# Head scores of a graph attention layer: four products into four banks instead of two pairs into two, with a new order of stages

## The reference

```python
x = _layernorm(x + L0(x, adj))   # one attention over the graph, softmax, elu
x = _layernorm(x + L1(x, adj))   # three times: attention, layer norm, feed-forward 256-1024-256 with gelu, layer norm
x = _layernorm(x + L2(x, adj))   # as L0, but only the 16 largest weights of each row are kept
x = _layernorm(x + L3(x, adj))   # eight heads of 32 features
```

```python
q, k, v = heads(x @ Wq), heads(x @ Wk), heads(x @ Wv)      # 8 heads, DK = 32
scores = einsum('bhnd,bhmd->bhnm', q, k) / sqrt(32)
scores = where(mask, scores, -inf)
out = einsum('bhnm,bhmd->bhnd', softmax(scores), v)
return relu(out) @ Wo
```

## Time and profile of the kernel before

| | |
|---|---|
| median of 3 timed runs | 4183.35 us (4180.52 to 4186.57) |
| profiled execution | 4172.75 us |
| its span, first to last instruction | 4171.1 us |
| mean granted TensorE clock | 0.927 |
| busy: TensorE, VectorE, ScalarE, GpSimd | 3650.7, 2396.8, 2176.5, 698.0 us |
| products of the heads' scores (L1183) | 1024 instructions, 315.6 us busy |
| transposes of the heads (L1195) | 2048 instructions, 360.8 us busy |

### The profile page before, as it was taken

One profiled execution on the slowest core, in us unless ns is written; L12 is line 12 of the kernel. 1 busy time (PEld: TensorE's weight loads), 2 busy tenths in 40 slices (PEclk: granted clock), 3 DMA queues, 4 the chain that ended last, 5 costly groups with the idle time before them and its releaser, 6 DMA issues.

```text
span 4171.1 us, 60266 instructions
## 1 busy us (share of the span) xinstructions
PE 3650.7 (88%) x18816; PEld 2758.4 (66%) x18816; DVE 2396.8 (57%) x6645; ACT 2176.5 (52%) x4321; POOL 698.0 (17%) x684
## 2 busy tenths in 40 slices
PE   6789898898988989899898998989898898998867
PEld 5676666766666676676766666666666766667653
DVE  3365564656656565565656656565565655646543
ACT  2255555455654555555554555555555554554623
POOL 1212121211111112121111212111121121212110
PEclk8799999998999999999999999989999998999987
DMA  4000000000000000000000000000000000000000
GB/s 120 1 6 6 6 11 7 11 1 6 11 7 11 6 2 10 7 11 6 6 6 7 11 6 11 4 4 11 6 11 7 6 6 6 11 6 1 1 5 6
DMA packets 42353, 39.73 MB, mean 10 GB/s; under 512 B 10016, under 2 KB 40992, under 8 KB 42016
## 3 DMA queue, kind: packets, MB, share of 16 engines
q1 hardware_dynamic: 33568, 27.17, 2.2%
q0 software_dynamic: 8448, 8.39, 1.4%
HBM read 35.55 MB, written 8.39 MB: 11 GB/s over the span
## 4 chain that ended last, share of the span: by engine, by line
PE 70%; issue 13%; DVE 8%; ACT 7%; POOL 2%; DVEq 0%; DMA 0%; ACTq 0%; POOLq 0%; SPq 0%
PE work L1133 16%; PE acc L1147 15%; PE acc L1111 11%; PE acc L1195 6%; PE work L1183 5%; PE work L1056 4%; PE work L1097 3%; PE acc L1213 2%; PE work L1162 2%; PE work L1026 2%; ACT PT L976 2%; PE work L1069 1%; DVE stats L692 1%; POOL rstd L477 1%; ACT T L907 1%
## 5 line engine op out<-in xcount | busy, mean ns | idle before, releaser
L1133 PE MATMUL work<-XT,w_sb 128*128 128x256 f32 x3072 | 759.2, 394 | 53.7 <-DVE XT L749 46.1
L477 POOL TENSOR_TENSOR rstd<-var_eps,minus_half 128x2 f32<-128x2 f32 x320 | 224.7, 702 | 3297.8 <-DVE var_eps L701 3297.8
L1147 PE MATMUL acc<-w_sb,gT 128*128 128x256 f32 x3072 | 716.6, 380 | 0.0
L1133 PEld LDWEIGHTS work<-XT,w_sb 128*128 128x128 f32 x3072 | 580.5, 196 | 182.9 <-DVE XT L749 44.4
L1147 PEld LDWEIGHTS acc<-w_sb,gT 128*128 128x128 f32 x3072 | 573.8, 190 | 85.1 <-issue 11.4
L947 ACT ACTIVATE gT<-work,b_sb 128x256 f32<-128x256 f32 x768 | 352.5, 473 | 365.9 <-PE work L1133 363.6
L1111 PE MATMUL acc<-X,PT 128*128 128x256 f32 x1536 | 392.6, 412 | 55.1 <-ACT PT L915 36.8
L1111 PEld LDWEIGHTS acc<-X,PT 128*128 128x128 f32 x1536 | 309.0, 207 | 128.1 <-issue 58.3
L810 DVE COPY PT<-acc 128x512 f32<-128x512 f32 x256 | 176.9, 691 | 292.3 <-PE acc L1195 288.1
L1183 PE MATMUL work<-X,R 32*128 32x512 f32 x1024 | 315.6, 663 | 19.3 <-DVE X L787 19.3
L976 ACT ACTIVATE PT<-acc 128x512 f32<-128x512 f32 x256 | 152.5, 596 | 297.2 <-PE acc L1195 295.2
(11 more groups left out here) (128 smaller groups left out, 5871.1 us busy)
## 6 DMA issues: line engine op xcount, KB each, us to landing
HX<-in_x SPq DMA_DIRECT2D x16, 512.0 KB, 3.9
pos<-in_adj POOLq DMA_DIRECT2D x16, 512.0 KB, 5.5
out<-X SPq DMA_DIRECT2D x32, 256.0 KB, 2.1
w_sb<-in_L_gnn_W SPq DMA_DIRECT2D x6, 1024.0 KB, 8.0
g_sb<-in_L_gnn_g SPq DMA_DIRECT2D x6, 128.0 KB, 5.1
c_sb<-in_L_gnn_beta SPq DMA_DIRECT2D x3, 128.0 KB, 4.1
PT<-in_L_gnn_b SPq DMA_DIRECT2D x3, 128.0 KB, 5.4
beta_sb<-in_L_gnn_beta SPq DMA_DIRECT2D x1, 384.0 KB, 7.8
```

The source lines that it names most:

```text
L477: pool.tensor_tensor(rstd[s][:, half_rows(half)], var_eps[s][:, half_rows(half)], minus_half[:], ALU.pow)\
L1133: last = pe.matmul(u.bank[:, 0:HN], w1_sb[:, l, c, f * P:(f + 1) * P], XT[s][:, c, half * HN:(half + 1) * HN], start=(c == 0), stop=(c == ...
L1147: last = pe.matmul(acc[s][half][:, i, :], gT[s][:, f, i * P:(i + 1) * P], w2_sb[:, l, f, :], start=(f == 0 and i == 0), stop=(f == FC - 1) ...
```

## The change

The 16 duos of a batch become 8 "quads" (`QUADS`, `NQ`): the four heads of a chunk for one tile of rows. Stage `sq{q}` multiplies all four into `acc[s][0]`, `acc[s][1]`, `work[s][0]`, `work[s][1]`; VectorE reads the first two banks in `sq{q}` and the other two in `sr{q}`. The four transposes of a quad go to the four banks as well, one each (`place_of` turns them by one where an output holds `acc[0]`). Each group of outputs has a bank use of its own, 256 columns: groups 0 to 2 in `acc[0]`, copied out by ScalarE with a Relu (`pc0` to `pc2`), group 3 in `acc[1]`. The spreading of the reciprocals comes at the end for both chunks (`rt0`, `rb0`, `rt1`, `rb1`); `rb0` is read by VectorE straight from its bank. A class `HeadUse` gives bank and semaphores for place 0 to 3.

```diff
-    DUOS = [(m, half, i, duo) for m in range(DC) for half in range(2) for i in range(HT) for duo in range(HPC // 2)]
+    QUADS = [(m, half, i) for m in range(DC) for half in range(2) for i in range(HT)]
...
+        for q in range(NQ):
+            uses += ([(f"scores {q + 1}", 2)] if q + 1 < NQ else []) + [(f"pT {q}", 2)]
+        uses += [("rden 1", 2)]
...
+        for q in range(NQ):
+            if q + 1 < NQ:
+                for h in range(2):
+                    acc_uses[h] += [(f"scores {q + 1}", 1)]
+            if q % 2 == 0 and q:
+                acc_uses[0] += [(f"outputs {q // 2 - 1}", 1)]
+            if q + 1 == NQ:
+                acc_uses[1] += [("rdenT 0", 1)]
+            for h in range(2):
+                acc_uses[h] += [(f"pT {q}", 1)]
+        acc_uses[0] += [("rden 0", 1), ("L3", 1)]
+        acc_uses[1] += [(f"outputs {GROUPS - 1}", 1), ("L3", 1)]
...
-        def bank_of(n):
-
-            return 1 if n < later else 0
+        def place_of(q, r):
+
+            return (r + 1) % HPC if q % 2 == 0 and q else r
...
+        class HeadUse:
+
+
+            def __init__(self, s, it, place, name):
+                if place < 2:
+                    self.bank = flat(acc[s][place])
+                    self.filled, self.filled_at = acc_filled[place].sems[s], acc_filled[place].value(it, name)
+                    self.evacuated, self.done = acc_evacuated[place].sems[s], acc_evacuated[place].value(it, name)
+                    self.free = acc_evacuated[place].value(it, name) - 1
+                else:
+                    u = Use(s, it, name, place - 2)
+                    self.bank, self.filled, self.filled_at = u.bank[:], u.filled, u.turn
+                    self.evacuated, self.free, self.done = u.evacuated, u.turn, u.turn + 1
...
+            def heads_normed(s, it, key):
+
+                last = Use(s, it, "rden 1", 1)
+                dve.wait_ge(last.evacuated, last.turn + 1)
+                outputs = HeadUse(s, it, 0, f"outputs {GROUPS - 2}")
+                dve.wait_ge(outputs.evacuated, outputs.done)
+                dve.tensor_tensor(XT[s][:, 1, 0:HN], XT[s][:, 1, 0:HN], chunks(R[s][:])[:, 1, 0:HN], ALU.mult)
+                use = HeadUse(s, it, 0, "rden 0")
+                dve.wait_ge(use.filled, use.filled_at)
+                dve.tensor_tensor(XT[s][:, 0, :], XT[s][:, 0, :], use.bank, ALU.mult).then_inc(use.evacuated, 1)
...
+            def group_outputs(g):
+                m, half = g // 2, g % 2
+
+                def stage(s, it, key):
+                    use = HeadUse(s, it, 0, f"outputs {g}")
+                    act.wait_ge(use.filled, use.filled_at)
+                    act.activation(XT[s][:, m, half * HN:(half + 1) * HN], use.bank[:, 0:HN], ACT.Relu).then_inc(use.evacuated, 1)
+                return stage
...
-                    for b in range(2):
-                        use = Use(s, it, f"scores d{d}", b)
-                        pe.wait_ge(use.evacuated, use.turn)
+                    places = [HeadUse(s, it, r, f"scores {q}") for r in range(HPC)]
+                    for use in places:
+                        pe.wait_ge(use.evacuated, use.free)
...
-                    for b in range(2):
-                        use = Use(s, it, f"scores d{d}", b)
-                        rows = slice((2 * duo + b) * DK, (2 * duo + b + 1) * DK)
-                        pe.matmul(use.bank[:], q_sb[s][rows, m, t * P:(t + 1) * P], k_sb[s][rows, m, :],
+                    for r, use in enumerate(places):
+                        rows = slice(r * DK, (r + 1) * DK)
+                        pe.matmul(use.bank, q_sb[s][rows, m, t * P:(t + 1) * P], k_sb[s][rows, m, :],
                                   start=True, stop=True).then_inc(use.filled, 1)
```

The list `HALF` is new as a whole. Its part with the heads, as it is now:

```diff
+        ("middle", "L1.0", "xsum1 xnorm1 xa1"), ("ending", "L3", "load qk0"), ("middle", "L1.1", "xT1"),
+        ("ending", "L3", "sq0"), ("middle", "L1.1", "s bc"), ("ending", "L3", "sr0"), ("middle", "L1.1", "zs0"),
+        ("ending", "L3", "v1"), ("middle", "L1.1", "mx0 zs1 exp0 mx1"), ("ending", "L3", "qk1"),
+        ("middle", "L1.1", "exp1 pT0"), ("ending", "L3", "ex0"), ("middle", "L1.1", "pT1"),
+        ("ending", "L3", "ex1 sq1 ex2 ex3"), ("middle", "L1.1", "agg0"),
+        ("ending", "L3", "sr1 uT0 ex4 uT1 ex5 uT2 ex6 uT3"), ("middle", "L1.1", "pT2 pT3"),
+        ("ending", "L3", "ex7 sq2 uT4"), ("middle", "L1.1", "sum0"), ("ending", "L3", "ex8 sr2"),
+        ("middle", "L1.1", "norm0"), ("ending", "L3", "uT5"), ("middle", "L1.1", "agg1"),
+        ("ending", "L3", "ex9 uT6"), ("middle", "L1.1", "hT0"), ("ending", "L3", "ex10 uT7"),
+        ("middle", "L1.1", "ha0 sum1 norm1 f100"), ("ending", "L3", "ex11 sq3"), ("middle", "L1.1", "f101"),
+        ("ending", "L3", "pv0"), ("middle", "L1.1", "hT1"), ("ending", "L3", "uT8"),
+        ("middle", "L1.1", "ha1 f102 f103 f200"), ("ending", "L3", "ex12 pc0 sr3 uT9 ex13 uT10 ex14 uT11"),
+        ("middle", "L1.1", "f110 f201"), ("ending", "L3", "ex15 sq4"), ("middle", "L1.1", "f111"),
+        ("ending", "L3", "uT12"), ("middle", "L1.1", "f202"),
+        ("ending", "L3", "ex16 sr4 uT13 ex17 uT14 ex18 uT15"), ("middle", "L1.1", "f112"),
+        ("ending", "L3", "ex19 sq5"), ("middle", "L1.1", "f203"),
+        ("ending", "L3", "pv1 rr0 uT16 ex20 pc1 sr5 uT17 ex21 uT18"), ("middle", "L1.1", "f113 xsum0"),
+        ("ending", "L3", "ex22 uT19"), ("middle", "L1.1", "xnorm0 xa0"), ("ending", "L3", "ex23"),
+        ("middle", "L1.1", "f210"), ("ending", "L3", "sq6"), ("middle", "L1.1", "f211"),
+        ("ending", "L3", "uT20 ex24 sr6 uT21"), ("middle", "L1.2", "xT0"),
+        ("ending", "L3", "ex25 uT22 ex26 uT23"), ("middle", "L1.1", "f212"), ("ending", "L3", "ex27"),
+        ("middle", "L1.1", "f213"), ("ending", "L3", "sq7 pv2"), ("middle", "L1.1", "xsum1"),
+        ("ending", "L3", "uT24 ex28 pc2 sr7 uT25 ex29 uT26 ex30"), ("middle", "L1.1", "xnorm1"),
+        ("ending", "L3", "uT27 ex31 rr1"), ("middle", "L1.1", "xa1"), ("ending", "L3", "rt0"),
+        ("middle", "L1.2", "xT1"), ("ending", "L3", "uT28 uT29 uT30 uT31 rb0 rt1"), ("middle", "L1.2", "s"),
+        ("ending", "L3", "rb1 hn0"), ("middle", "L1.2", "bc zs0"), ("ending", "L3", "proj0"),
+        ("middle", "L1.2", "mx0 zs1 exp0 mx1"), ("ending", "L3", "pv3"), ("middle", "L1.2", "exp1 pT0"),
+        ("ending", "L3", "hn1 ysum0"), ("middle", "L1.2", "pT1"), ("ending", "L3", "norm0 proj1"),
+        ("middle", "L1.2", "agg0 pT2"), ("ending", "L3", "ysum1"), ("middle", "L1.2", "pT3"),
```

More of the change, by code:

```diff
@@ L788, in keys, with head_scores @@
                 return stage
-            def head_scores(d):
-                m, half, i, duo = DUOS[d]
+            def head_scores(q, part):
+                m, half, i = QUADS[q]
                 def stage(s, it, key):
-                    for b in range(2):
-                        n = 2 * d + b
-                        use = Use(s, it, f"scores d{d}", b)
-                        dve.wait_ge(use.filled, use.turn)
+                    for r in range(2 * part, 2 * part + 2):
+                        n = HPC * q + r
+                        use = HeadUse(s, it, r, f"scores {q}")
+                        dve.wait_ge(use.filled, use.filled_at)
                         hold(dve)
-                        dve.tensor_tensor_reduce(score_tile(s, n), use.bank[:], pos0[s][:, half * HT + i, :], 1.0, HIGHEST,
+                        dve.tensor_tensor_reduce(score_tile(s, n), use.bank, pos0[s][:, half * HT + i, :], 1.0, HIGHEST,
                                                  ALU.add, ALU.min, head_min[s][:, n:n + 1]).then_inc(use.evacuated, 1)
@@ L849, in _ @@
             stages |= {f"pT{t}": weights_transposed(t) for t in range(NT)}
-            stages |= {f"sc{d}": head_scores(d) for d in range(ND)}
+            stages |= {f"sq{q}": head_scores(q, 0) for q in range(NQ)} | {f"sr{q}": head_scores(q, 1) for q in range(NQ)}
             stages |= {f"uT{n}": head_transposed(n) for n in range(NK) if n % 2}
@@ L1001, in _ @@
                       "qk0": queries(0), "qk1": queries(1),
-                      "rt0": rden_transposed(0), "rt1": rden_transposed(1), "rb0": rden_broadcast(0), "rb1": rden_broadcast(1)}
+                      "rt0": rden_transposed(0), "rt1": rden_transposed(1), "rb1": rden_broadcast}
+            stages |= {f"pc{g}": group_outputs(g) for g in range(GROUPS - 1)}
             stages |= {f"f1{h}{q}": gelu(h, q) for h in range(2) for q in range(4)}
@@ L1165, in project_transposed, with head_scores @@
                 return stage
-            def head_scores(d):
-                m, half, i, duo = DUOS[d]
+            def head_scores(q):
+                m, half, i = QUADS[q]
                 def stage(s, it, key):
-                    if d % (ND // DC) == 0:
+                    if q % (NQ // DC) == 0:
                         for name in "qk":
@@ L1187, in head_transposed @@
             def head_transposed(n):
-                m, half, i, duo = DUOS[n // 2]
```

(36 more changed lines are left out.)

102 lines of the change are left out of this document (45 added, 57 removed), and 79 rows, old and new, of the table HALF.

## The result

The changed kernel takes 3895.64 us (median of 4 runs, 3883.13 to 3898.82) against 4181.94 us of the kernel before (4176.26 to 4186.57): ratio 0.9307, 95% interval 0.9281 to 0.9333, 286 us less. I had forecast 140 us less, 4043 us, with a range down to 3970. The direction was right, the size was half of what came.

The account below looks back on a forecast made before the run. The prediction took TensorE to bound each half batch, with 25 to 28 us idle in it. Its terms, -143 - 12 - 61 + 32 + 8 + 36 = -140 us, from 4183.35 gave 4043 us, range 3970 to 4145.

Parts of the forecast that it names:

- Products: Heads' products on TensorE: a quad takes 1.18 us instead of two pairs' 2.30, -143 us (bounds -147 and 0).
- the entries (-12): Weight loads before the heads' products: half of the entries into the mode go, 0.1 us each, -12 us (bounds 0 and -42).
- Transposes: Heads' transposes through four banks no longer wait for the copy before: half of 122.7 us idle, -61 us (bounds -123 and 0).
- the clock comes along: Rival: with denser queues in 1164 to 1220 us, halves become like those of 245.8 us; 3964 us, chance 0.12.
- New waits: TensorE waits before and behind quad 2, covered at most others: 2 us a batch, +32 us (bounds 0 and +282).
- the quad holds the queue: Rival: each quad waits for the last copy, transposes behind it for VectorE's reads; +66 us, 4249 us, chance 0.09.
- The order elsewhere: Stages moved past a half's end, behind proj0 or between the heads: costed at nothing (bounds -79 and +101 us).
- Given back: Less cover for the other batch's late norms: a quarter of the products' gain lost, +36 us (0 to 143).
- Table loads: ScalarE changes between Gelu and Exp: 24 a half instead of 22, 41 us, a fifth seen, +8 us (bounds 0 and 41).
- two by two: Rival: a quad's four products run side by side only in twos, so the products gain 0; 4150 us, chance 0.04.
- the other batch's chain: Rival: the middle batch's chain of norms sets a half, so gaps only move; -42 us, 4141 us, chance 0.15.

Follow-up runs that it names:

- quads_twice: The changed kernel with each quad's four products issued twice into the same banks; 4001.13 us, ratio 0.9578, 105 us over the changed kernel.
- serial_transposes: The changed kernel, but TensorE waits before each of the heads' transposes for the copy of the one before; 4246.86 us, ratio 1.0157.
- the short copies: The kernel before, with copies of the heads' transposes carrying 128 of 512 columns (outputs not the reference's); 4077.19 us, ratio 0.9749.
- short copies, old banks and new order: The kernel before, its duos and banks in the new order, with transpose copies of 128 columns instead of 512; 4328.54 us, ratio 1.0338.
- quads_early: The changed kernel with quads 3 to 7 directly behind a last transpose, ahead of the f1 and f2 stages that stood between; 4005.79 us, ratio 0.9571.
- new_heads_old_rest: The changed kernel with the new order only in the stretch with the heads, the order of before ahead of it; 3891.48 us, ratio 0.9306.
- pv3_first: The changed kernel with the last group of outputs (pv3) ahead of proj0 instead of behind it; 3892.14 us, ratio 0.9309.

## Why the prediction was wrong, point by point

By the account, with my terms put together as it cuts them (the wait of a transpose behind a quad counts for the products, the wait of a quad for the stage ahead of it):

```
                                                    forecast   measured
products, with the waits behind a quad (-143 +16)     -127       -136
transposes (-61)                                       -61       -144
all else: entries, quads' waits, loads, given back
  (-12 +16 +8 +36)                                     +48         +5
sum                                                   -140       -275 of the profiled executions
```

- **Products: right.** A quad holds the queue 1.07 us. I took 1.09 at full clock; the estimate by the 3.07 of the Trainium skill, "TensorE: Matmul & The Clock Gate", section "Measured speedup vs the span model", was 1.20. quads_twice shows that this time counts one for one. What the entries (-12) brought can't be told apart.
- **Transposes: this step failed.** I wrote: "Of the 122.7 us the first transpose behind an exponential or behind a quad still waits. I take half: -61 us (bounds -123 and 0)." The kinds of wait were right, and idle time did fall by 72 us. The error was to take booked idle time as the price, and as the bound too: the transposes' line fell by 144 us, past the bound of 123. First, a wait costs more than is booked. A duo before, TensorE alone:

```profile
1120.83 0.66 PE L1195 MATMUL acc<-ident,T 128*128 128x128 f32 x4
1122.17 0.66 PE L1195 MATMUL acc<-ident,T 128*128 128x128 f32 x4 [0.69 <-ACT PT L976]
1122.76 1.13 PE L1183 MATMUL work<-X,R 32*128 32x512 f32 x4
```

  From 1120.83 to 1122.76 are 1.93 us (2.99 - 1.06 in the earlier trace rows), against 0.87 for two transposes back to back: 1.06 us for a wait booked at 0.69. A transpose that stands alone has a record of 0.66 us, and the queue is held 0.43 where another follows; idle time starts at the record's end and hides 0.2 us of the stall. The other 0.16 us are the second transpose, which holds the queue 0.59 before the pair. Second, before the change 103 of the transposes' 441 us ran at 1.2 GHz, and 0.2 of 297 after it: at most 51 us of the 144, so at least 92 are stalls. I had the two halves of 245.8 and 258.6 us at different clocks and made that a rival of its own ("the clock comes along", 3964 us, chance 0.12); both came, in the same stages. That stalls of the transposes can lower their clock is seen in serial_transposes (82 us of theirs at 1.2 GHz again); what brought the kernel before to 103 stays open, since the short copies left 101 of them.
- **The exchange rate** can be read off pairs of profiled executions that differ in waits of the heads. "Idle" is what is booked before the instructions named:

```
                                              idle      time    ratio   clock
short copies before (transposes)             -56.2       -96     1.7    0.927 -> 0.936
transposes made to wait (and quads)         +195.9      +342     1.7    0.946 -> 0.922
short copies, old banks and new order        -87.3      -198     2.3    0.893 -> 0.922
quads early (quads, transposes, outputs)     +81.8      +110     1.3    0.946 -> 0.944
```

  By all of TensorE's idle time (-61.5, +189.9, -100.0, +88.8) the ratios are 1.6, 1.8, 2.0 and 1.2. In the one pair where the clock hardly moves, a booked us costs 1.2 to 1.3; where it moves along, 1.6 to 2.3.
- **New waits: small before the quads, as forecast, larger behind them.** Idle time before the quads is 26.3 us (I expected 30 to 50, by the copies; 11.5 us of it are the copies', against the 16 I took). The cover by f1 and f2 that I read off the order is confirmed by quads_early, which takes it away. Behind quad 2 its first transpose waits for VectorE's read as forecast (0.92 us, 14.9 in all). But I had counted pv2 as cover behind quad 7, and pv2 writes into `acc[0]`, which that quad has just filled:

```profile
1107.98 1.93 PE L1254 MATMUL acc<-PT,V 128*32 128x256 f32 x32 [0.92 <-DVE head_min L826]
1109.85 0.66 PE L1235 MATMUL acc<-ident,T 128*128 128x128 f32 x4
1111.46 1.33 PE L1235 MATMUL work<-ident,T 128*128 128x128 f32 x8 [0.95 <-DVE head_min L826]
```

  So it waits itself (14.9 us in all), and uT25 behind it as well (14.3): 29 us that my +32 did not hold. I also read the cover ahead of the quads once too often: it stands ahead of five, and agg0 stands behind quad 1. The rival "the quad holds the queue" is a true mechanism, and the old order with new banks shows it (117.8 us booked before the quads). It was wrong for this order.
- **The order elsewhere: zero, as taken**, shown by new_heads_old_rest but for the four moved stages, and by pv3_first for pv3. But I took the order within the heads as a neutral carrier too. It is not: neither banks nor order gain alone.
- **Given back: wrong.** I let the middle batch's norms take back a quarter of the products' gain. Waits did move: idle time before the f1 stages and the transposes of x and h rose by 60 us, that before pT and agg fell by 103. But the other stages took back 5 us in all, and quads_twice shows nothing given back between the two speeds of the products.
- **Table loads: the number right, the price not tested.** 30 more (366 for 336, at 1.28 us each); ScalarE's busy time rose by 28 us. TensorE's idle time until a Gelu ended rose from 12.6 to 26.6 us; how much of that the loads make, no run shows.

Of the two rivals with a smaller gain, "two by two" (4150 us) fell with the quad's 1.07 us, and "the other batch's chain" (4141 us) with the one-for-one rate.

## What to carry to other kernels

A stall of the bounding engine can cost more than the idle time booked before it (here 1.2 to 2.3 times): read its price from the distance of starts, with and without the stall, and ask what it does to the clock before setting an upper bound. When buffers and the order of a queue change together, cost them together; the same banks came with -286 or +108 us by the order they were walked in. A burst that needs all banks is cheap if one stage of other work stands between the last instruction whose result is still to be read and the burst, and another behind it that needs none of these banks.

## What the runs showed of the hardware

- Four float32 products of 32 rows and 512 columns, in four quarters and four banks, take the queue 1.07 us, as two do (1.06); one after another they would take 3.69 (an estimate, by the q and k row): 3.4 times as fast. The first passes of the four start within 0.01 us. A second set right behind adds 0.85 us (quads_twice). The Trainium skill, "TensorE: Matmul & The Clock Gate", section "Measured speedup vs the span model", has 3.07 for the same shape; the measurement here is higher.
- Relu on ScalarE (the copies pc0 to pc2) brought no table load of its own: loads are booked at Gelu, the heads' and the layers' exponentials:

```profile
L982 ACT ACT_TABLE_LOAD x183 | 234.8, 1283 | 3.2
L1000 ACT ACT_TABLE_LOAD x90 | 115.5, 1283 | 1.6
L963 ACT ACT_TABLE_LOAD x60 | 77.0, 1283 | 0.3
L942 ACT ACT_TABLE_LOAD x33 | 42.3, 1283 | 2.1 <-DVE neg_max L663 1.6
```

- The transposes with the stalls of one bank ran partly at the granted clock 0.5 (103 us), the same transposes without them hardly ever (0.2 us); where the stalls between transposes were put back (serial_transposes), the mean clock fell to 0.922. Idle time alone does not decide it: quads_early adds 98 us of it before the quads, and the mean clock stays at 0.944. What does, these runs don't show.
